# An expert stage written out without loops on three engines, its expert numbers packed five to a word

## The reference

```python
xn = _layernorm(x, axis=-1)
s = _L0_attn_ref(xn, ...)          # causal, two softmaxes a head, one times lambda subtracted
g = _silu(_L0_ffn_ref(xn, ...))
x = x + s * g
# of _L0_ffn_ref, with T = 4096 tokens, E = 8 experts, TOP_K = 2, H = I = 256:
logits = h @ router_weight.T + router_bias
top_vals, top_idx = jax.lax.top_k(logits, TOP_K)
top_w = jax.nn.softmax(top_vals, axis=-1)
gate_up = jnp.einsum('th,ehj->etj', h, gate_up_proj) + gate_up_proj_bias[:, None, :]
gate = jnp.minimum(gate_up[..., ::2], LIMIT)
up = jnp.clip(gate_up[..., 1::2], -LIMIT, LIMIT)
act = (up + 1.0) * gate * jax.nn.sigmoid(gate * ALPHA)
expert_out = jnp.einsum('eti,eih->eth', act, down_proj) + down_proj_bias[:, None, :]
out = jnp.einsum('te,eth->th', scores, expert_out)
```

## Time and profile before

| | us |
| --- | --- |
| median of 3 runs (1091.31 to 1091.75) | 1091.36 |
| the profiled execution's own time | 1086.14 |
| its span, first to last instruction | 1084.4 |
| TensorE busy, share of the span | 932.2 (86%) |
| VectorE busy | 938.8 (87%) |
| ScalarE busy | 769.4 (71%) |
| GpSimd busy | 284.1 (26%) |

### The profile page before, as it was taken

The page is one execution under the profiler, slowest core; times in us unless marked ns, Lnnn a source line. Parts: engine busy times, 40 slices in busy tenths (PEclk is TensorE's granted clock), DMA queues, the critical chain, the costliest instruction groups (busy, mean ns, idle before and its releaser), DMA issues. The chain is left out here.

```text
span 1084.4 us, 25051 instructions
## 1 busy us (share of the span) xinstructions
PE 932.2 (86%) x6626; PEld 652.0 (60%) x6627; DVE 938.8 (87%) x1857; ACT 769.4 (71%) x1982; POOL 284.1 (26%) x478
## 2 busy tenths in 40 slices
PE   4999968898988999898989898987999999993665
PEld 3877745666666666666666666664565556552444
DVE  6777858999999999999999999993777777775997
ACT  3545437999999999999999999993333333335673
POOL 3000001233333333331000000023666666651000
PEclk9999996999999999999999999998999999996788
DMA  6988966666857586756855564611222222225454
GB/s 220 326 305 288 318 255 132 143 140 142 188 134 153 138 188 143 156 130 129 117 117 123 110 133 99 141 19 39 82 82 83 82 82 82 82 73 170 155 177 132
DMA packets 89630, 157.52 MB, mean 145 GB/s; under 512 B 19613, under 2 KB 48797, under 8 KB 89565
## 3 DMA queue, kind: packets, MB, share of 16 engines
q1 hardware_dynamic: 80544, 137.52, 50.0%
q0 software_dynamic: 9056, 19.67, 5.9%
HBM read 104.66 MB, written 52.49 MB: 145 GB/s over the span
## 5 line engine op out<-in xcount | busy, mean ns | idle before, releaser
L1144 DVE TENSOR_REDUCE nmax<-bank 128x1 f32<-128x1024 f32 (+3 forms) x256 | 260.3, 1017 | 6.6 <-PE bank L976 6.6
L1077 ACT ACTIVATE Pr_long<-bank,nmax 128x1024 f32<-128x1024 f32 (+3 forms) x256 | 251.9, 984 | 9.9 <-DVE nmax L1144 9.8
L1104 ACT COPY AT<-bank 128x512 f32<-128x512 f32 (+3 forms) x384 | 177.0, 493 | 3.8 <-PE bank L1015 1.8
L974 PE MATMUL bank<-Ks_first,Qs_first 128*128 128x512 f32 (+3 forms) x384 | 124.0, 413 | 28.8 <-ACT Pr_short L1091 19.6
L1091 ACT ACTIVATE Pr_short<-bank,nmax 128x128 f32<-128x128 f32 (+3 forms) x256 | 138.3, 540 | 9.4 <-DVE nmax L1162 1.5
L1349 PE MATMUL bank<-gu_sb,xsT 128*128 x288 | 141.0, 613 | 3.0 <-DVE hid L1453 0.5
L1015 PE MATMUL bank<-ident,Pr_long 128*128 128x128 f32 x832 | 127.6, 280 | 18.4 <-DVE Pr_long L1194 18.2
L847 POOL COPY VO<-Ob 128x64 f32 (+1 forms) x128 | 30.3, 237 | 414.7 <-ACT Ob L1113 414.3
L1194 DVE SCALAR_TENSOR_TENSOR Pr_long<-Pr_long,coef 128x1024 f32<-128x1024 f32 (+3 forms) x128 | 137.6, 1075 | 0.0
L974 PE MATMUL bank<-Ks_second,Qs_second 128*128 128x512 f32 (+3 forms) x384 | 119.7, 400 | 20.1 <-ACT Pr_short L1091 19.9
L976 PE MATMUL bank<-maskb,identb 128*128 128x128 bf16 x512 | 117.8, 233 | 0.0
(11 more groups left out here) (162 smaller groups left out, 1692.6 us busy)
## 6 DMA issues: line engine op xcount, KB each, us to landing
q_parts<-PARTS SPq DMA_DIRECT2D x32, 512.0 KB, 3.5
k_parts<-PARTS SPq DMA_DIRECT2D x32, 512.0 KB, 4.4
Qs_first<-q_parts SPq DMA_DIRECT2D x64, 256.0 KB
Ks_first<-k_parts SPq DMA_DIRECT2D x64, 256.0 KB
Qs_second<-q_parts SPq DMA_DIRECT2D x64, 256.0 KB
Ks_second<-k_parts SPq DMA_DIRECT2D x64, 256.0 KB
yg<-y_dram SPq DMA_DIRECT2D x16, 512.0 KB, 5.4
X<-x SPq DMA_DIRECT2D x8, 512.0 KB, 6.0
```

What stands on the lines that cost most here:

```text
L974: nc.tensor.matmul(at[:, c0:c1], Qs[head][:, m, q * P:(q + 1) * P], Ks[head][:, m, c0:c1], start=True, stop=(c1 < N))
L1077: nc.scalar.activation(long_probs(p)[:, m, 0:N], long_slot[m][:, 0:N], ACT.Exp, bias=nmax[:, 4 * p + m:4 * p + m + 1], scale=1.0, accum_ou ...
L1104: nc.scalar.copy(AT[u % 6][:, 0:w], tb[u % BANKS][:, 0:w]).then_inc(unit_out, 1)
L1144: nc.vector.tensor_reduce(nmax[:, 4 * p + m:4 * p + m + 1], long_slot[m][:, 0:N], AX.X, ALU.max, negate=True).then_inc(long_maxed, 1)
```

## The change

`run_steps` has no loop any more. On TensorE, VectorE and ScalarE it writes out all 72 steps, in the order in which they stood, in 9 blocks of 8 tiles. All semaphore values are thereby constants.

The table is now `expert_words`: for each block of eight tiles two words, each the sum of five expert numbers times 1, 8, 64, 512 and 4096 (3 bits each), so that the two words hold the experts of the eight tiles and of the two after them. `load` reads the two words of a block once, into two new registers, and takes an expert out of a word by a shift and a mask of the register where it is used. In routing VectorE clips the numbers into a scratch of floats, multiplies by `place_of`, sums by fives, and converts the sums to whole numbers. `place_of` is five more constants that GpSimd sets at the start; `consts_done` is therefore waited for at 11.

```diff
--- before.py
+++ after.py
@@ -34,6 +34,9 @@
 TOP_K = 2
 SLOT_TILES = T * TOP_K // P + E
 KB_UNIT = 4
+BLOCK = 8
+PER_WORD = (BLOCK + 2) // 2
+EXPERT_BITS = 3
 
 
 def credited(it, per, event):
@@ -176,8 +179,12 @@
         tot = routing(NT * E).rearrange("p (t e) -> p t e", e=E)
         per_e = routing(5 * E).rearrange("p (i e) -> p i e", e=E)
         rcmp = routing(SLOT_TILES * (E + 1))
-
-        expert_rows = sb("expert_rows", [P, SLOT_TILES // 2, 4], I32)
+        place_of = routing(PER_WORD)
+        word_sums = routing(SLOT_TILES // BLOCK * 2)
+        in_block = routing(SLOT_TILES // BLOCK * (BLOCK + 2)).rearrange("p (i n) -> p i n", n=BLOCK + 2)
+
+
+        expert_words = sb("expert_words", [P, SLOT_TILES // BLOCK, 4], I32)
 
 
         Qs_first = sb("Qs_first", [P, 2, S], F32R)
@@ -306,6 +313,8 @@
                     nc.gpsimd.affine_select(out=earlier[:], in_=earlier[:], compare_op=ALU.is_gt, fill=0.0,
                                             base=0, pattern=[[1, P]], channel_multiplier=-1
                                             ).then_inc(consts_done, 1)
+                    for n in range(PER_WORD):
+                        nc.gpsimd.memset(place_of[:, n:n + 1], float(1 << EXPERT_BITS * n)).then_inc(consts_done, 1)
                     nc.gpsimd.tensor_copy(count_f, count_i[:]).then_inc(const_step, 1)
                     pool.wait_ge(const_step, 16)
                     nc.gpsimd.tensor_scalar(count_128, count_f[:, 0:T // P], float(P), None, ALU.mult
@@ -488,7 +497,7 @@
                     low_weights(0)
                     low_rows(0, 0)
                     low_weights(1)
-                    dve.wait_ge(consts_done, 6)
+                    dve.wait_ge(consts_done, 6 + PER_WORD)
 
                     dve.wait_ge(w_loaded, 80)
                     nc.vector.tensor_tensor(lam_w[:], lam_in[:, 0:4:2, :], lam_in[:, 1:4:2, :], ALU.mult
@@ -542,11 +551,17 @@
                     then(nc.vector.tensor_tensor(cs, end.unsqueeze(1).broadcast_to([P, SLOT_TILES, E]),
                                                  count_f.unsqueeze(2).broadcast_to([P, SLOT_TILES, E]), ALU.is_le))
                     then(nc.vector.tensor_reduce(rcmp[:, SLOT_TILES * E:], cs, AX.X, ALU.add))
-                    pairs = rcmp[:, SLOT_TILES * E:].rearrange("p (i u) -> p i u", u=2)
-                    NR = SLOT_TILES // 2
-                    nc.vector.tensor_scalar(expert_rows[:, :, 0:2], pairs, float(E - 1), None, ALU.min)
-                    nc.vector.tensor_scalar(expert_rows[:, 0:NR - 1, 2:4], pairs[:, 1:], float(E - 1), None, ALU.min)
-                    nc.vector.memset(expert_rows[:, NR - 1:NR, 2:4], 0)
+                    of_tile = rcmp[:, SLOT_TILES * E:].rearrange("p (i n) -> p i n", n=BLOCK)
+                    NR = SLOT_TILES // BLOCK
+                    nc.vector.tensor_scalar(in_block[:, :, 0:BLOCK], of_tile, float(E - 1), None, ALU.min)
+                    nc.vector.tensor_scalar(in_block[:, 0:NR - 1, BLOCK:], of_tile[:, 1:, 0:2], float(E - 1), None,
+                                            ALU.min)
+                    then(nc.vector.memset(in_block[:, NR - 1:NR, BLOCK:], 0.0))
+                    words = in_block.rearrange("p i (w n) -> p (i w) n", n=PER_WORD)
+                    then(nc.vector.tensor_tensor(words, words, place_of.unsqueeze(1).broadcast_to(
+                        [P, 2 * NR, PER_WORD]), ALU.mult))
+                    then(nc.vector.tensor_reduce(word_sums, words, AX.X, ALU.add))
+                    nc.vector.tensor_copy(expert_words[:, :, 0:2], word_sums.rearrange("p (i w) -> p i w", w=2))
 
                     dve.wait_ge(odds_ready, 1)
                     then(nc.vector.tensor_scalar(top[:, 3], top[:, 4], 1.0, None, ALU.add))
@@ -641,7 +656,7 @@
                         pe.sem_inc(xn_stored[h], 16)
                     for i in range(QKT):
                         pe.sem_inc(parts_stored[i], 16)
-                    pe.wait_ge(consts_done, 6)
+                    pe.wait_ge(consts_done, 6 + PER_WORD)
 
                     def turn_rows(b, h):
                         b, h = b + h // 2, h % 2
@@ -1296,12 +1311,18 @@
 
                 def expert_loader(eng):
 
-                    registers = [eng.alloc_register(f"expert{n}") for n in range(4)]
+                    loads = [0]
 
                     def load(i):
-                        eng.load(registers, expert_rows[0:1, bass.ds(i, 1), :].rearrange("p o n -> p (o n)"))
-                        return [bass.RuntimeValue.of_register_unchecked(r, min_val=0, max_val=E - 1)
-                                for r in registers]
+
+                        registers = [eng.alloc_register(f"experts{loads[0]}_{n}") for n in range(2)]
+                        loads[0] += 1
+                        eng.load(registers, expert_words[0:1, bass.ds(i, 1), 0:2].rearrange("p o n -> p (o n)"))
+                        words = [bass.RuntimeValue.of_register_unchecked(r, min_val=0,
+                                                                         max_val=(1 << EXPERT_BITS * PER_WORD) - 1)
+                                 for r in registers]
+                        return [((words[n // PER_WORD] >> EXPERT_BITS * (n % PER_WORD)) & (E - 1)
+                                 ).with_bounds(min_val=0, max_val=E - 1) for n in range(BLOCK + 2)]
 
                     return load
 
@@ -1313,15 +1334,13 @@
 
                 def run_steps(eng, step, load=None):
 
-                    load = load or (lambda it: None)
+                    load = load or (lambda j: None)
                     step(0, 0, load(0))
-                    with eng.Fori(0, NIT3 - 2) as it:
-                        e = load(it)
-                        step(it, 1, e)
-                        step(it, 2, e)
-                    e = load(NIT3 - 2)
-                    for n in (1, 2, 3, 4):
-                        step(NIT3 - 2, n, e)
+                    last = SLOT_TILES // BLOCK - 1
+                    for j in range(last + 1):
+                        e = load(j)
+                        for n in range(1, BLOCK + 1):
+                            step(j * (BLOCK // 2), n, e)
 
                 def turn_rows(it, n):
 
```

## The result

The changed kernel took 1079.99 us (median of 4 runs, 1078.88 to 1080.42), the kernel before beside it 1091.34 (4 runs, 1089.14 to 1091.75): a ratio of 0.9903, 95% interval 0.9891 to 0.9915. The forecast was 1080.2. The same pair was measured twice more, on other chips: 0.9918 (0.9905 to 0.9932) and 0.9916 (0.9901 to 0.993). Taken together the gain is some 9 to 11 us, a little less than the 11.13 of the forecast, and two of the three intervals leave out the 0.9898 that it meant.

A forecast was written before the change was run, and what follows sets the result against it. TensorE was taken to bound the expert stage, waiting for its own sequencer once a loop round. Removing the seams saves 11.13 us, all other terms 0: 1091.36 - 11.13 = 1080.2 us, range 1078.8 to 1087.1.

The forecast's parts named there:

- the 11.13 of the forecast: Expert stage, third to last tile: 219.51 us falls to 208.38 at 3.02 a tile, saving 11.13 us.
- The bound and its cause: Expert stage: TensorE sets the pace; its sequencer's loop end and load make it late, 0.33 us lost a round.
- The load: TensorE's two-word load at 8 block seams costs 0, hidden by queued work; bounds 0 and 2.7 us.
- Shift and mask: TensorE's chain behind the xsT_ready wait: added register instructions fit by 0.07 us, cost 0; bounds 0 to 0.2 a tile.
- Rival (a): Shift and mask do not fit TensorE's chain: 1087.1 us partly, 1094.0 fully; chance 0.09 partly, 0.05 fully.
- VectorE: Expert stage: its bias add starts 0.2 us later, but its 2.83 us turn stays below 3.02; cost 0.
- Rival (d): Expert stage: another engine holds 3.18 us a tile, so 1091, no change; chance 0.04.
- Rival (b): Expert stage: TensorE waits for straight code to be fetched; 1084.2 us partly, 1093.0 fully; chance 0.08 partly, 0.03 fully.
- rival (c): TensorE's loop seams: only the taken branch was worth something, gain 4.4 us, 1087.0; chance 0.03.
- The first tiles: Start of the expert stage: a jump, MOVE and FUSED_REGOPS leave TensorE's sequencer path; at most 0.1 us, counted 0.
- The sum: Whole kernel: 11.13 us off the median 1091.36 gives 1080.2; off the profiled 1086.14 gives 1075.0.

The follow-up runs named there:

- tensor_alone: Changed kernel with straight steps on TensorE only, ScalarE and VectorE keeping the loop of before; 1079.85 us, ratio 0.9929 to the kernel before.
- others_alone: The reverse: ScalarE and VectorE straight and packed, TensorE keeping its loop and four numbers a round; 1089.4 us, ratio 1.0017 to the kernel before.
- straight_unpacked: Changed kernel without packing: straight steps on three engines, four numbers loaded every two tiles, no shift or mask; 1078.01 us, ratio 0.9902.
- loop_of_eight: Changed kernel's packed words, but a loop of 8 rounds of eight tiles on the three engines, last eight behind it; 1084.12 us, ratio 0.9964.
- two_more_masks: Changed kernel with two more register masks that change nothing for every expert number TensorE uses; 1083.97 us, ratio 0.9966.
- after_third: The changed kernel, unchanged, run for a third trace; 1076.26 us (one run), expert stage 208.95 us.
- before_again: The kernel before, unchanged, run for a second trace; 1088.36 us (one run), third to last tile 219.48 us.

## Why the prediction was right, step by step

**The bound and its cause held.** TensorE set the pace, its sequencer was late once a round, and without the branch the seam is gone. tensor_alone and others_alone show it.

**The 11.13 us were 10.56.** Of the 0.57 between, 0.22 belong to the 58th tile, which ends a block and stands behind GpSimd's pause: its load starts 0.3 us later than the others, at 923.1, and the slack is not enough. The fourth and the twelfth have 0.07 each. 0.1 is the third tile's product, which starts late and lasts 1.98 in every trace, and 0.1 the 3.02 itself, rounded: straight_unpacked has 208.59 without a long tile.

**The load: 0 was right, its reason was not.** The row that it leaned on was a load of four words, 338 ns, and "the same instruction with more words" was taken to be the upper bound. Two words take 536. The forecast also took that one load, behind a branch not taken, for the way of all: of straight_unpacked's 37 only the first is longer than 343 ns, but at the same place in loop_of_eight a load took 724 for 536. The load of two words still hides, but with 0.07 us to spare (at the block's end at 850.2 the last address instruction starts at 851.14 and takes its turn of 0.1 us, the weight load starts at 851.30): in tensor_alone, where it starts 0.4 us later, it costs 0.3 to 0.4 at a seam, and 0.6 with a long load.

**Shift and mask fit,** by 0.10 us instead of 0.07 (two_more_masks, and 0.11 by the disturbed tiles). Rival (a) fell. Their price shows elsewhere, in executions that are disturbed.

**VectorE.** VectorE idles 0.35 us before its bias add (829.42, above) for 0.27 in the earlier trace rows; nobody waited for it, as forecast. Rival (d) fell in the changed kernel, and has a small part in tensor_alone.

**The straight code is fetched without a wait.** DMA queue 8, whole run and then the stretch from 743 to 966 us of after_third:

```profile
q8 instruction: 20, 0.33, 0.1%
```

```profile
q8 instruction: 10, 0.16, 0.3%
```

9 packets more than before, of 16 KB each; the forecast had 8 by the rows. In after_third the products at 760.62 and 784.86, each less than 0.1 us late, start 0.6 us ahead of a packet; beside the other eight packets of the stage the tiles take 3.02 to 3.03 us. Straight_unpacked fetches its code in the same way and has no long tile. Rival (b) fell, and rival (c) with the even seams. The Trainium skill, Runtime: NRT & Kernel Launch, section "Instruction fetch mechanics", has blocks of 16 KiB, or 256 instructions, from which the forecast estimated nine. The trace agrees, with 9 packets of 16 KB.

**The first tiles** came out at nothing, but by two parts. The first product stands 1.08 us behind the second transposes instead of 0.79 (744.03 to 744.82 before), since the first load takes 719 ns for 522; by the third tile it is made good. After_third:

```profile
746.21 0.69 PE L1354 MATMUL bank<-ident,xs_second 128*128 128x128 f32 x2 [1.93 <-DMA xs_second<-xn_dram,slot_tokens]
747.29 4.95 PE L1368 MATMUL bank<-gu_sb,xsT 128*128 x8 [0.39 <-issue]
```

**What no step had: attention, 0.8 us longer.** VectorE's row maxima over all of attention, before_again and after_third:

```profile
L1144 DVE TENSOR_REDUCE nmax<-bank x256: 807/1016/1225, 165.0 to 731.4; 128x1 f32<-128x1024 f32 x32, 128x1 f32<-128x896 f32 x32, 128x1 f32<-128x768 f32 x32, 128x1 f32<-128x640 f32 x32
```

```profile
L1159 DVE TENSOR_REDUCE nmax<-bank x256: 805/1016/1225, 164.3 to 731.5; 128x1 f32<-128x1024 f32 x32, 128x1 f32<-128x896 f32 x32, 128x1 f32<-128x768 f32 x32, 128x1 f32<-128x640 f32 x32
```

566.4 and 567.2 us. The whole difference arises at one place, 29 us into the stage. VectorE and GpSimd there, before_again:

```profile
194.59 0.33 DVE L1206 SCALAR_TENSOR_TENSOR Pr_short<-Pr_short,coef 128x128 f32<-128x128 f32 x1
194.83 0.21 DVE L1181 SCALAR_TENSOR_TENSOR coef<-dsum,lam_s,rec 128x2 f32<-128x2 f32 x1
...
194.93 0.73 POOL L872 TENSOR_TENSOR gub_sb<-gub_sb 128x256 f32<-128x256 f32 x1
```

and after_third:

```profile
193.74 0.64 DVE L1221 SCALAR_TENSOR_TENSOR Pr_short<-Pr_short,coef 128x128 f32<-128x128 f32 x1
194.30 0.75 DVE L1196 SCALAR_TENSOR_TENSOR coef<-dsum,lam_s,rec 128x2 f32<-128x2 f32 x1
...
193.50 0.73 POOL L887 TENSOR_TENSOR gub_sb<-gub_sb 128x256 f32<-128x256 f32 x1
194.31 0.73 POOL L888 TENSOR_TENSOR gub_sb<-gub_sb 128x256 f32<-128x256 f32 x1
```

VectorE's two operations take 1.39 us instead of 0.54. Each ends 0.0 to 0.2 us behind an operation of GpSimd that ran beside it from its start (194.23 and 194.38; 195.04 and 195.05). Before, GpSimd comes to this place 0.1 us behind the second one's start. Why it comes earlier now is not settled. All the kernels run here but the one before have it, others_alone and loop_of_eight too, so it doesn't take TensorE's straight code; what all of them share is the longer routing, with five more constants and the packed table, and it was not tested by itself. The Trainium skill, SBUF — State Buffer, section "Terms", has the port pair that VectorE and GpSimd share as an exclusive lock held for a whole instruction. The trace agrees, with 0.33 turned to 0.64 and 0.21 to 0.75.

**The sum** by what was measured: 10.56 - 0.8 = 9.8 us. The three pairs of medians give 11.35, 8.81 and 9.59. That the first landed within 0.3 us of the forecast owes something to scatter: the oversized 11.13 met an execution set that favoured the change. For a profiled execution the prediction had 1075.0: the first one took 1080.42, with its disturbances, and after_third 1076.26. Taking the gain off the median and not off the profiled execution was right: before_again and after_third have spans of 1086.6 and 1074.5, far from the first pair's 1084.4 and 1078.7.

## What to carry to other kernels

Where the engine that sets the pace loses time to its own sequencer, write its steps out, and write out those of its feeders as well: an in-order sequencer that waits for a late feeder runs into its own loads late. Count the slack of the shortest chain before putting instructions on it, since an even trace hides what a disturbed execution will charge. Don't pack words to save loads before the loads are seen to cost anything: here the table of before with straight steps was the faster kernel, by 2.5 us beside the changed one on a disturbed chip and by 0.36 in the stages of two even traces.

## What was not expected of the hardware

- A load of two words from SBUF into registers takes 536 ns on TensorE's sequencer, one of four words 333. Both take 0.2 us more when they are the first of the stage, and on TensorE in most rounds of a loop. The taken branch isn't the cause, or not alone: 724 ns behind a branch not taken, 539 and 333 behind taken ones, and 671 and 700 in straight code.
- A taken branch lasts 208 ns on TensorE, 56 on VectorE and 45 on ScalarE (medians in loop_of_eight).
- In four traces, three of them from one chip, TensorE's semaphores reach the engines that wait for them up to 1.5 us late, seven to twelve times in 210 us, longest near the same two tiles. What it is stays open.
- One operation of GpSimd at the wrong moment took two short ones of VectorE to two and three and a half times their length.
